# A four-layer graph network on one core: a new preparation, and a norm's scaling moved from VectorE to ScalarE in the second edge pass

## The reference, cut to what matters

```
x = layernorm(x + L0(x, edge_attr, edges))     # 16 heads, tanh edge gates, MLP with its own norm and relu
x = layernorm(x + L1(x, edges))                # 4 heads, self loops; gelu(norm(out + bias) * gamma + beta)
x = layernorm(x + L2(x, edges))                # two GATv2 layers, elu, a linear layer
x = layernorm(x + L3(x, edges, edge_attr))
```

```
out = out + bias
mu, var = mean(out), mean((out - mu)^2)
out = (out - mu) * rsqrt(var + 1e-5) * gamma + beta
return gelu(out)
```

## Time and profile before

| | us |
|---|---|
| median of 3 runs (3929.29 to 3931.96) | 3930.91 |
| the profiled execution | 3930.92 |
| its span in the trace | 3929.2 |
| preparation, 0 to 68 | 68 |
| node pass | 1161 |
| edge pass "0" | 562 |
| edge pass "1", 1791 to 2352.3 | 561.3 |
| edge passes "2a", "2b", "3" | 533, 500, 541 |

### The profile page before, as it was taken

One profiled execution on the slowest core, in us unless ns is written; L12 is line 12 of the kernel. 1 busy time (PEld: TensorE's weight loads), 2 busy tenths in 40 slices (PEclk: granted clock), 3 DMA queues, 4 the chain that ended last, 5 costly groups with the idle time before them and its releaser, 6 DMA issues. The chain is left out here.

```text
span 3929.2 us, 70937 instructions
## 1 busy us (share of the span) xinstructions
PE 3463.5 (88%) x19239; PEld 2424.3 (62%) x19434; DVE 3443.5 (88%) x6459; ACT 2988.0 (76%) x10008; POOL 2266.1 (58%) x2305
## 2 busy tenths in 40 slices
PE   2999999999995999996999978999969999678775
PEld 2888888888883666664666644545535555355443
DVE  3899999999995999996999977999969999699886
ACT  1999999999994999984898875666648888454443
POOL 1577777777776777624555505444334443477777
PEclk9999999999997999998999998999979999899998
DMA  1455555555554444423554425555535555455442
GB/s 47 124 156 146 152 156 149 149 156 148 149 151 116 113 113 113 106 80 107 129 127 124 126 55 143 139 145 139 127 100 155 157 158 156 110 141 143 123 121 72
DMA packets 719118, 503.42 MB, mean 128 GB/s; under 512 B 141745, under 2 KB 621335, under 8 KB 718960
## 3 DMA queue, kind: packets, MB, share of 16 engines
q1 hardware_dynamic: 533072, 362.39, 33.7%
q0 software_dynamic: 56528, 81.64, 8.5%
q10 hardware_dynamic: 129360, 57.82, 5.3%
HBM read 304.28 MB, written 200.10 MB: 128 GB/s over the span
## 5 line engine op out<-in xcount | busy, mean ns | idle before, releaser
L237 ACT ACTIVATE node_z<-psum 128x128 f32<-128x128 f32 x1568 | 419.0, 325 | 22.2 <-PE psum L217 13.1
L1204 POOL DMA_INDIRECT slot2a_src_rows<-x,src_table_cols x196 | 236.3, 1205 | 307.3 <-PE psum L226 178.6
L659 ACT ACT_TABLE_LOAD x305 | 391.3, 1283 | 5.4
L237 ACT ACTIVATION_READ_ACCUMULATOR node_z<-psum 128x1 f32 x1568 | 348.2, 227 | 0.0
L1204 POOL DMA_INDIRECT slot_src_rows<-x,map_cols x196 | 202.2, 1032 | 251.7 <-PE psum L226 124.6
L1204 POOL DMA_INDIRECT slot2b_src_rows<-xl,map_cols x196 | 190.5, 972 | 232.8 <-PE psum L226 186.5
L237 ACT ACTIVATE slot_logit<-psum 128x128 f32<-128x128 f32 x980 | 256.5, 278 | 85.7 <-PE psum L217 55.6
L1208 POOL DMA_INDIRECT slot_dst_rows<-in_x,dst_gather_cols x196 | 213.5, 1090 | 120.6 <-PE psum L226 59.7
L1204 POOL DMA_INDIRECT slot_src_rows<-x,src_table_cols x196 | 203.4, 1038 | 127.4 <-POOLq L250 68.0
L1014 POOL DMA_INDIRECT node_gathered<-in_x,src_cols x196 | 236.2, 1205 | 47.1 <-issue 47.1
L1238 POOL DMA_INDIRECT out_nodes<-slot_new,out_index x196 | 217.9, 1112 | 60.1 <-issue 60.1
(11 more groups left out here) (422 smaller groups left out, 12070.4 us busy)
## 6 DMA issues: line engine op xcount, KB each, us to landing
x<-node_x SPq DMA_DIRECT2D x294, 256.0 KB, 3.0
slot_neg<-neg SPq DMA_DIRECT2D x147, 256.0 KB, 4.9
node_xT<-in_x_T SPq DMA_DIRECT2D x98, 256.0 KB, 3.1
out_nodes<-node_x SPq DMA_DIRECT2D x98, 256.0 KB, 2.8
x<-slot_new ACTq DMA_DIRECT2D x98, 256.0 KB, 2.4
slot_keep<-keep SPq DMA_DIRECT2D x98, 256.0 KB, 4.2
slot_dst_rows<-x SPq DMA_DIRECT2D x98, 256.0 KB, 5.4
xl<-node_xl SPq DMA_DIRECT2D x98, 128.0 KB, 2.7
```

The source lines that it names most:

```text
L237: ins = act.activation(g.z[u][:, t, :], rows[:, t, :], ACT.Square, scale=float(D ** -0.5), accum_out=sums[u][:, t:t + 1])
L659: act.add_instruction(mybir.InstLoadActFuncSet(name=nc.get_next_instruction_name(), ins=[], outs=[], act_func_set_id=wanted[0]))
L1204: pool.indirect_dma_start(src_rows[u][:, t, 0:src_width], None, table, at_index(rows[:, tile, 0:1], 0))\
```

## The change

1. Preparation. The list of loads is split in three groups with a semaphore each ("rows", "first", "late"), ordered anew, and issued by SP (33) and ACT (27). The loads are 60: four broadcasts to 128 partitions (`raw_b1`, `raw_b2`, `raw_bias`, `raw_bl2`) are replaced by columns. DVE and PE begin as soon as the group that they need has arrived: the first slots with "rows", centring and bias columns with "first", the rest with "late". POOL makes the identity first, and the map's DMA last.
2. Bias rows. The five biases are columns of one 128x5 tile; their centring is one product with `center`; the three bf16 levels are casts and subtractions of 128x5 tiles; one product with a bf16 identity turns the 15 columns to rows, and one copy writes them four times side by side to `bias_levels`. `pe_rows` multiplies `level_of[:, k, :]` (128x128, ones in the three rows of bias k, zeros elsewhere) with `bias_levels` (128x512, for `bl2` 4 x 64 columns of it). It has 128 rows and the same columns as before.
3. Pass "1". `z1` goes from DVE to ACT, as four scalings of 128x128, and PE's `z1T` waits for ACT. The plan has new times for all steps.

```diff
-        pe.matmul(bank(u)[:, 0:TILES * width], g.c.ones[:, 0:P], bias[:, 0:TILES * width], start=True, stop=False)
+        levels = tiles_of(g.c.bias_levels[:, :])[:, :, 0:width]
+        pe.matmul(bank(u)[:, 0:TILES * width].rearrange("p (t n) -> p t n", t=TILES), g.c.level_of[:, ROW_BIASES.index(bias), :], levels,
+                  start=True, stop=False)
...
+    by_sp = loads["rows"] + loads["first"][0::2] + loads["late"][0::2]
+    by_act = loads["first"][1::2] + loads["late"][1::2]
...
-            v.wait_ge(loaded, 16 * len(loads))
+            v.wait_ge(arrived["rows"], everything["rows"])
...
+            v.wait_ge(arrived["first"], everything["first"])
...
+            n = did(v.tensor_copy(bias_parts[:, :, 0], biases[:, :]))
+            n = did(v.tensor_tensor(bias_rest[0][:, :], biases[:, :], bias_parts[:, :, 0], ALU.subtract))
...
+            v.wait_ge(arrived["late"], everything["late"])
...
+            did(v.tensor_copy(tiles_of(c.bias_levels[0:LEVELS, :]), psum[0:LEVELS, 6, 2 * D:3 * D].unsqueeze(1).broadcast_to([LEVELS, TILES, D])))
...
+            pe.matmul(psum[0:LEVELS, 6, 2 * D:3 * D], bias_parts[:, :, :].rearrange("p k l -> p (k l)"), ident_half[:, :],
+                      start=True, stop=True).then_inc(levels_ready, 1)
...
-        "1": [("PE", "h1")] + slot_norm("sq2", "z1", False) + [("PE", "z1T"), ("ACT", "gelu1"), ("PE", "y1")] +
+        "1": [("PE", "h1")] + slot_norm("sq2", "z1", False, scaled_by="ACT") + [("PE", "z1T"), ("ACT", "gelu1"), ("PE", "y1")] +
...
+                elif step == "z1":
+                    act.wait_ge(*g.ACT.done(u, i, "sq2_rstd"))
+                    for t in range(TILES):
+                        ins = act.activation(g.z[u][:, t, :], A(u)[:, tile_cols(t)], ACT.Copy, scale=g.raw[u][:, t:t + 1])
+                    ins.then_inc(g.act_out[u], 1)
...
-                    pe.wait_ge(*g.DVE.done(u, i, "z1"))
+                    pe.wait_ge(*g.ACT.done(u, i, "z1"))
```

More of the change, by code:

```diff
@@ L190 @@
 UNCOUNTED = ("store", "gather", "put", "dst_gather", "scatter")
+ROW_BIASES = ("b1", "b2", "bias", "bl2", "xlr")
+LEVELS = 3 * len(ROW_BIASES)
 def tiles_of(t):
@@ L288, in sb, with fetch, load, column @@
         return ctx.enter_context(nc.sbuf_tensor(name, shape, dt))
-    loads = []
-    def load(name, shape, src, dt=F32, room=None):
+    loads = {"rows": [], "first": [], "late": []}
+    def fetch(into, src, group):
+        loads[group].append((into, src))
+    def load(name, shape, src, dt=F32, room=None, group="late"):
         t = (room or sb)(name, shape, dt)
-        loads.append((t[:], src))
+        fetch(t[:], src, group)
         return t
[L297 to L301, removed]
+    def column(name, src, m=P, group="late"):
+        return load(name, [m, 1], src.rearrange("(p o) -> p o", o=1), group=group)
     own = ExitStack()
@@ L312, in prepare @@
     c.We0, c.We1 = sb("We0", [P, D]), sb("We1", [P, D])
[L313 to L333, removed]
+    fetch(c.We0[0:EF, :], a["L0_gnn_We0"], "late")
+    fetch(c.We1[0:EF, :], a["L0_gnn_We1"], "late")
+    c.dst_gather_cols = load("dst_gather_cols", [P, SLOT_TILES], a["dst_gather_cols"], I32)
     c.ident = sb("ident", [P, P])
@@ L367, in prepare @@
     c.payload = sb("payload", [P, SLOT_TILES, 2], I32)
[L370 to L381, removed]
+    row_here = [load(f"row_here{o}", [SLOT_CHUNKS, CHUNK], a["dst_rows"][o], I32, temp, "rows") for o in range(2)]
+    row_prev = [load(f"row_prev{o}", [SLOT_CHUNKS, CHUNK], a["dst_prev_rows"][o], I32, temp, "rows") for o in range(2)]
+    raw = {n: load("raw_" + n, [P, D], src, room=temp, group="first") for n, src in (
+        ("W1b", a["L0_gnn_W1"][D:2 * D, :]), ("W2", a["L0_gnn_W2"]), ("W1a", a["L0_gnn_W1"][0:D, :]))}
+    raw_cols, wide_bl2 = temp("raw_cols", [P, 3]), temp("wide_bl2", [P, 1])
+    for k, src in enumerate((a["L0_gnn_b1"], a["L0_gnn_b2"], a["L1_gnn_bias"])):
+        fetch(raw_cols[:, k:k + 1], src.rearrange("(p o) -> p o", o=1), "first")
+    fetch(wide_bl2[0:C2, :], a["L2_gnn_bl2"].rearrange("(p o) -> p o", o=1), "first")
+    raw_blin = load("raw_blin", [P, D], a["L2_gnn_blin"].partition_broadcast(P), room=temp, group="first")
+    br1 = load("br1", [P, 1], a["L2_gnn_br1"].rearrange("(p o) -> p o", o=1), room=temp, group="first")
+    here = [load(f"here{o}", [P, SLOT_TILES], a["dst_cols"][o], I32, temp) for o in range(2)]
+    after = [load(f"after{o}", [P, SLOT_TILES], a["dst_next_cols"][o], I32, temp) for o in range(2)]
     vectors = {}
@@ L388, in prepare @@
         for h in range(4):
[L389 to L394, removed]
+            fetch(vectors[n][32 * h:32 * h + 32, :], a["L3_gnn_a"][h:h + 1, 32 * k:32 * k + 32].rearrange("o c -> c o"), "late")
+    br2_twice, att2_twice = temp("br2_twice", [P, 1]), temp("att2_twice", [P, 1])
+    for half in (0, C2):
+        fetch(br2_twice[half:half + C2, :], a["L2_gnn_br2"].rearrange("(p o) -> p o", o=1), "late")
+        fetch(att2_twice[half:half + C2, :], a["L2_gnn_att2"].rearrange("h (c o) -> (h c) o", o=1), "late")
+    raw["Wn"] = load("raw_Wn", [P, D], a["L3_gnn_W_node"], room=temp)
+    raw_edge = load("raw_edge", [P, EF], a["L3_gnn_W_edge"], room=temp)
     pair_gap = temp("pair_gap", [P, D])
@@ L428, in _ @@
             with nc.allow_non_contiguous_dma("a few vectors"):
-                for dst, src in loads:
-                    sp.dma_start(dst, src).then_inc(loaded, 16)
+                for item in by_sp:
+                    sp.dma_start(*item).then_inc(arrived[group_of[id(item)]], 16)
             sp.wait_ge(masks, 4)
@@ new lines, in _ @@
+            v.wait_ge(worked, n)
+            for k in range(len(to_center)):
+                n = did(v.bn_aggr(mean[:, k, :], stats[:, k, :]))
+            v.wait_ge(worked, bias1_at)
+            did(v.tensor_scalar(c.value_bias1[:, :], c.node_bias1[:, :], 1.0, None, ALU.add))
+            v.wait_ge(sums_ready, 1)
+            did(v.tensor_copy(biases[:, 0:3], psum[:, 6, D:D + 3]))
+            did(v.tensor_copy(biases[:, 3:4], wide_bl2[:, :]))
+            biases_at = did(v.tensor_tensor(biases[:, 4:5], wide_bl2[:, :], psum[:, 6, 0:1], ALU.subtract))
@@ new lines, in _ @@
+            marks["src_float"] = count[0]
+            flags_at = [did(v.tensor_tensor(c.last[o][:, :], here[o][:, :], after[o][:, :], ALU.not_equal)) for o in range(2)][0]
+            v.wait_ge(levels_ready, 1)
+            did(v.tensor_copy(tiles_of(c.bias_levels[0:LEVELS, :]), psum[0:LEVELS, 6, 2 * D:3 * D].unsqueeze(1).broadcast_to([LEVELS, TILES, D])))
+            v.wait_ge(worked, n)
+            did(v.tensor_scalar(c.own_relu[:, :], c.S1[:, :], SLOPE - 1.0, None, ALU.mult))
+            did(v.tensor_scalar(c.src_relu[:, :], c.S1[:, :], 1.0 - SLOPE, None, ALU.mult))
@@ L633, in _ @@
-            ins.then_inc(products, 1)
+            pe.wait_ge(made, marks["ident"])
             pe.wait_ge(firsts, 2)
```

335 lines of the change are left out of this document (175 added, 160 removed), and 16 rows, old and new, of the table PLAN.

## The result

| | before | changed kernel |
|---|---|---|
| median of the runs, us | 3931.3 (5 runs) | 3914.9 (5 runs, 3905.9 to 3916.1) |
| ratio | 1 | 0.9953, 95% interval 0.9941 to 0.9966 |
| profiled execution, us (span) | 3930.9 (3929.2) | 3915.5 (3913.8) |

What follows compares the result with a forecast made beforehand. Load issuing followed by a DVE list bounds the preparation, DVE bounds pass "1". 3930.9 - 35.5 (preparation) + 5.5 (pass "1") = 3900.9 us; own range 3892 to 3910, 8 in 10 3884 to 3919.

Steps and rivals of the forecast that it cites:

- The preparation, 35.5 saved: Preparation: two queues issue loads side by side and early work hides behind them, 32.5 us against 68.0.
- Rival (a): Preparation: two queues share one rate, loads arrive no sooner; 23.5 saved instead of 35.5, total 3912.9; chance 0.13.
- The bias products, 0: PE's bias products: same rows and columns, reading bl2 in four pieces costs nothing; 0 us change.
- The other stages equal to within 2 us: Stages outside preparation and pass "1", node pass included: lengths unchanged to within 2 us.
- Pass "1", +5.5: Pass "1": 21.1 per pair, 0.2 more, over 23 periods +4.6, drain +0.9; 566.8 us.
- I estimate 0.7 in all: Pass "1", ACT: the new order gives back 0.7 us per pair, lowering ACT's floor from 21.4 to 20.7.
- The chain: Pass "1": PE works 6.0 us without a gap against ACT's 5.7, so ACT waits 0.3 to 0.4 per pair.
- DVE's floor of 19.7: Pass "1": losing two z1 gives DVE back 1.2 us per pair, from 20.9 to 19.7.
- (c): Pass "1": three engines above 94% wait for each other in turn, 0.7 us per pair more; 3917; chance 0.14.
- (b): Pass "1": DVE's relief comes through, ACT closes without waits, floor as low as 20.4; 3885; chance 0.11.
- (d): Pass "1": z1 on ACT stalls the ring; slower from 1.5 us per pair, 3953 with 2.5; chance 0.05.
- (e): Whole kernel: no effect where meant, parts small and stage barriers keep gains; 3929; chance 0.04.

Runs made afterwards that it cites:

- e11: The kernel before with the new preparation and bias products, but all 60 loads issued by SP; pass "1" as before: 3902.7 us (ratio 0.9933).
- e6: The changed kernel with pass "1" in its old order, z1 still on ACT, right behind its reciprocal root: 3919.7 us.
- e7: The changed kernel with z1 back on DVE, pass "1" otherwise in the new order: 3920.5 us (one run).
- e4: The changed kernel with z1 as one ACT step using one column's scale for all four tiles (values wrong): 3897.3 us (ratio 0.9916).

## Why the prediction was right, and where it was off

- *The preparation, 35.5 saved.* The mechanism was right, 39.8 measured, just outside the 29 to 39 that I gave it. The loads' issuing was the bound, and two queues run fully beside each other: 0.51 us an issue, not the 0.55 I took, and the last one had landed at 19.7, not 22.4: it took 2.1 us from the end of its issue, not 3.4. DVE's late list took 8.0 us for 39 instructions, 0.205 each, near the busy time alone (0.199) that stood as the lower end. The two together were the 38.9 of my end. Rival (a), one rate, is refuted by e11 as well.
- *The skill's rule on issuing engines* stood beside that. It holds here as far as it says that only the sequencer's time is saved; that this is usually small does not hold: it was 13.5 of 41.4 us.
- *The bias products, 0.* Right: 273 ns for 256 columns before and after.
- *"The other stages equal to within 2 us."* Wrong for the node pass, +9.9. I had a list of what could lengthen it with one entry, the `bl2` pieces. Where ScalarE's instructions lie was no item of my sum. Over all profiles, six without the long issues at that place have node passes of 1161.0 to 1164.7 us (mean 1162.8), eight with them 1167.0 to 1172.2 (mean 1169.4): 6.6 us of the 9.9 are this, and the rest lies within the scatter. By the turns the two groups are further apart: 79.15 to 79.30 us a turn in the six, 79.56 to 79.78 in the eight.
- *Pass "1", +5.5.* The direction was right, the size was not: +17.1, and 21.5 per pair in place of 21.1. z1's cost on ACT holds: four steps take 1.12 to 1.14, and in the old order ACT needs 21.5 (e6), where I had 19.3 + 2.1 = 21.4. The term that failed is "I estimate 0.7 in all" for what the new order gives back to ACT: it gives back 0.4, from 21.5 to 21.1, and nothing with the old work (e7: 21.99 less 2.7 of waits for others is 19.3 again). ACT's waits for others are 0.4 per pair, as forecast, but only 3.2/20.5 = 0.16 of them is the wait for h1, in every second pair; 0.25 is for DVE, which I hadn't counted. The chain failed where it says that PE does its part "without a gap": PE stands 0.38 us ahead of `r.a` for DVE's `fc` (row at 1981.11), in just those pairs in which ACT waits for h1, and they are the 21.66 ones.
- *DVE's floor of 19.7* was off as well. Without the two z1 DVE needs 20.5, not 20.9 - 1.2. In the window it is busy 37.83/40 x 21.5 = 20.3 us per pair. The forecast's 93 to 95% busy came true (94.6%) by luck: both the work and the period were larger. In e6, also without the two z1, DVE needs 20.3. Why it lost less than its two z1 was not tested; a step that had to wait can't overlap the one before it, as the prediction has it for ACT.
- *The rivals.* What happened in the pass lies between the forecast and (c), three engines lock: 0.4 per pair over my 21.1 where (c) had 0.7. That e4 gave back half of what was taken off ACT speaks for it: with ACT as the only bound it would have been all. (c) got a chance of 0.14. (b) was refuted: DVE was relieved (to 37.83 of 40), and the period grew. (d) did not come: PE waits 0.44 us per pair for z1 (8.8/20), far from 1.5. (e), no effect, is out by the interval.
- *The sum.* 4.3 better in the preparation, 9.9 + 11.6 worse in the two passes, 2.6 better elsewhere: 14.6 above, as measured (3915.5 against 3900.9). None of the four came out as its term had it; that the total is off by only 0.4% is in part luck, since two of them have the opposite sign.

## What to carry to other kernels

When one engine is at 100% and two others are at 90 to 95%, moving work off the first can make the stage longer, as here. Work out for each engine what it needs (the period less its waits for others), before and after, and look at how close the three come to each other: here they came within 1.0 us of the period, and of 0.9 us taken off one of them half went into its waits. An order of work is fitted to where the work is: here neither the moved work nor the new order could be priced without the other. After an edit ahead of a long loop, compare the loop's turns one by one: a stall of under 1 us in each can come from where the instructions lie, and here a few waits that were already met moved it away.

## What the runs showed of the hardware

- Records of instruction fetches lie at fixed places of ScalarE's node loop, some 110 to 150 recorded instructions apart, and move with the number of ScalarE instructions ahead of the loop (14 more: about 2 us earlier in a turn of 79.2 to 79.8) and not with SyncE's. A fetch that started inside a run of SyncE's issues, at 10 to 12 us of the turn, took 0.8 to 2.3 us, one at 15 us of the turn 0.3 to 0.5; the issue beside it took 0.8 to 1.9 us instead of 0.37 in 10 to 12 of 12 turns.
- Two queues issue side by side: 0.51 us an issue on SyncE with ScalarE issuing beside it at 0.54, 0.504 for SyncE alone.
- An engine's busy time isn't fixed by its list: PE has the same steps in pass "1" before and after and is busy 37.46 and 37.92 of 40 us, per pair 19.6 and 20.4 (the profile models the ends of PE's steps).
- Moving the node tiles by 32 bytes changed the mean time of the loads' and stores' 512-byte packets from 28.5 to 27.0 ns, and that of the 2048-byte packets from 99 to 141, and not the stage. The multiple of 64 isn't the reason for the 141: the kernel before has its tiles at one too, and there the means are 27.2 and 102.
- Open: the five times of the changed kernel fall in two groups, 3905.9 and 3906.8 against 3914.9 to 3916.1; the profile is of the second.
